# Last phase of a two-layer MetaFormer kernel: the back ring of PSUM banks goes from three banks to two

## The chip, the cores and the metric

The kernel runs on 1 core of one Trainium2 chip. The metric is device time in microseconds (us); lower is better. Engines are named as the profile names them: PE is TensorE's matmul, PEld its weight load, DVE is VectorE, ACT is ScalarE, POOL is GpSimd, SP is SyncE, which only issues transfers here. PSUM, the memory that PE writes, has eight banks in each partition; a matmul output sits in one bank, and DVE or ACT must read it out before PE may overwrite it.

## The reference: what is computed

The input is (8, 96, 128, 128). Two layers follow, each a token mixer and then a feed-forward network (FFN) with a hidden size of 384, both with a residual:

```
x = x + L0_conv(ln_c(x), ...)                      # layer 0: clustering mixer
t = to_tokens(x); t = t + L0_ffn(ln_t(t), ...); x = from_tokens(t)
x = x + L1_conv(ln_c(x), ...)                      # layer 1: convolutions, then pw * gate
t = to_tokens(x); t = t + L1_ffn(ln_t(t), ...); x = from_tokens(t)
# ffn: y = q_acc(q_mul(relu(q_acc(q_mul(x) W1) + b1)) W2) + b2, with fp8 and fp16 rounding
```

Layer 1's mixer ends with a 1x1 convolution (`pw_w`) whose result is multiplied by the normalised input of the mixer.

## The kernel before, in words

There are three phases: A (layer 0), B (depthwise convolutions of layer 1) and C (the 1x1 convolution, the gate, and the FFN of layer 1). Only phase C is touched. It runs from about 3025 us to the end.

Phase C works through 32 units (`NQ`) of 4096 tokens, each in 8 groups `k` of 512 tokens. A *step* `i` overlaps two units: the front work of unit q = i + 1 and the FFN of unit i. A step has 9 *slots*, s = 0 to 8 (`FFN_SLOTS`). The steps i = 0 to 30 have both kinds of work; step -1 has only front work and step 31 only the FFN. All engines run their own instruction streams strictly in the order written, and meet at semaphores.

In slot s each engine issues, in this order:

- PE: `q8` of group s+1 (four transposing matmuls, L1409), `hidden` of group s (three matmuls of 512 columns, L272), `pw` of group s (L1577), `turn` of group s-1 (four transposes, L1586), `c` of group s-1 (four transposes, L1596), `y` of group s-1 (three matmuls, L1423).
- ACT: the copy `q8c` of group s+1 (L296), the copy `h16` of `hidden` of group s (L307), in all slots but 1 four normalising activations (L1394), the copy `y16` of group s-1 (L1436).
- DVE: `hq` of group s (L229 three times, L233 once), `gate` of group s (L1653), `x4` of group s-1 (L1663), `y16b` of group s-1 (L1442), statistics (L178), and as its last instruction `out` of group s-1 (L1682), which reads the bank that `c` wrote.

Slots 7 and 8 are irregular. Slot 7 has no `q8`. Slot 8 has the `q8` of group 0 of the next unit, and no `hidden` and no `pw`. Slot 0 has no `turn`, `c`, `y`. Where a text here says "the end of DVE's slot", it means the end of that slot's `out`.

The bank that each PE group writes is given out by `Ring` in rotation. The list of uses is fixed: 24 uses of the back ring in a step (`q8`, `c`, `y`), 16 of the front ring (`pw`, `turn`). Use n takes bank n modulo the number of banks, and `Ring.before` names the use of that same bank just before it; PE then waits, before the first matmul of use n, for the event that says that the earlier use was read out. For `q8` that event is `q8c`, for `y` it is `y16` (both ACT), for `c` it is `out` (DVE). `hidden` has its own three banks (`C_hid`), used once per slot, so `hidden` of group s also waits for `h16` of group s-1. The 24 back uses in order, with s the slot, are: `q8`1 in slot 0; then in slots 1 to 6 `q8`(s+1), `c`(s-1), `y`(s-1); `c`6, `y`6 in slot 7; `q8`0 of the next unit, `c`7, `y`7 in slot 8.

Of the kernel before, what the change touches and what calls it, by code (L numbers as in the profile page):

```python
# [5 lines left out]
F32 = mybir.dt.float32  # L6
# [9 lines left out]
P = 128  # L16
# [1429 lines left out]
def phase_c(nc, consts, pw_t, w1, b1, w2, b2, x2_dram, x3_dram, y3_dram, out_dram):  # L1446
# [3 lines left out]
    with ExitStack() as ctx:  # L1450
        sb = lambda n, s, d: ctx.enter_context(nc.sbuf_tensor(n, s, d))
        sem = lambda n: ctx.enter_context(nc.semaphore(n))
        front_uses, back_uses = [], []
# [28 lines left out]
        gated = sb("C_gated", [C, 2, CH], F32)  # L1482
        outq = sb("C_outq", [C, RB, W], F32)
        front = Ring(front_uses, [ctx.enter_context(nc.psum_tensor(f"C_fbank{p}", [P, 512], F32)) for p in range(2)])
        back = Ring(back_uses, [ctx.enter_context(nc.psum_tensor(f"C_bbank{p}", [P, 512], F32)) for p in range(3)])
        ff = RowFeedForward(nc, ctx, "C_", ev, back, xT_flat, wts, idb)
        HR = RB // 2

# [251 lines left out]
def metaformer_kernel(nc, x, consts, wf_t, wf, bf, wv_t, bv, wp_t, bp, alpha, beta, w1_0, b1_0, w2_0, b2_0,  # L1740
                      gamma, beta_ln, taps, dwb, pw_t, w1_1, b1_1, w2_1, b2_1, out):
    x2_dram = nc.dram_tensor("x2_scratch", [NQ, P, NK * CW], F32, kind="Internal").ap()
    x3_dram = nc.dram_tensor("x3_scratch", [C, B, H, W], F32, kind="Internal").ap()
    y3_dram = nc.dram_tensor("y3_scratch", [C, B, H, W], F32, kind="Internal").ap()
    phase_a(nc, consts, x, wf_t, wf, bf, wv_t, bv, wp_t, bp, alpha, beta, w1_0, b1_0, w2_0, b2_0,
            gamma, beta_ln, x2_dram, x3_dram)
    phase_b(nc, taps, dwb, x3_dram, y3_dram)
    phase_c(nc, consts, pw_t, w1_1, b1_1, w2_1, b2_1, x2_dram, x3_dram, y3_dram, out)
# [54 lines left out]
```

## Time and profile before

| | |
|---|---|
| time, median of 3 runs | 4256.6 us (4250.14 to 4260.43) |
| profiled execution: time, span | 4258.63 us, 4256.8 us |
| mean granted clock of TensorE | 0.887 of full |
| busy over the span | PE 78%, DVE 71%, ACT 63%, POOL 33% |
| phase C, 3400 to 3800 us (400 us) | PE 315.85, DVE 334.19, ACT 336.51 us busy, clock 0.95 |

The time is 1.8 us more than the span. Busy shares are averages over phases with different limits, so phase C is to be read from its own stretch: there PE, DVE and ACT are each busy 79 to 84% of the time, and none is saturated. A granted clock of 1.00 is 2.4 GHz and one of 0.50 is 1.2 GHz; a value between is a stretch that held both.

### The profile page before, as it was taken

How to read it: one execution, taken by the hardware profiler on the slowest of the kernel's cores; microseconds unless marked ns; L12 is line 12 of the kernel's file. 1: busy time of each engine (PE TensorE's matmuls, PEld its weight loads, DVE VectorE, ACT ScalarE, POOL GpSimd, SP SyncE). 2: the span in 40 equal slices, each digit the busy share in tenths (PEclk: the TensorE clock that was granted, in tenths of full speed). 3: DMA queues.
4: the chain of work that ended last, by engine and by line, in shares of the span. 5: the costliest groups of instructions: out<-in, count | busy, mean ns of one | idle time of the engine just before them, and what ended most of it. 6: DMA issues, size and time to landing. Idle time of an engine off the chain costs nothing. (4 is left out here: it accounts for less than half of the span.)

```text
span 4256.8 us, 81198 instructions
## 1 busy us (share of the span) xinstructions
PE 3309.3 (78%) x26660; PEld 2549.8 (60%) x26660; DVE 3027.4 (71%) x7852; ACT 2686.4 (63%) x5250; POOL 1408.0 (33%) x1892
## 2 busy tenths in 40 slices
PE   6767777676776777767669999999788777778787
PEld 5556555555555555555549999999544444444443
DVE  4888888888888888888842222222388788778787
ACT  2567667676676776766752222222388788888887
POOL 3555555555555555555310000000022221212221
PEclk8888788888888887888879999999799999999998
DMA  3133232332323323222146656656766565666562
GB/s 62 44 75 83 67 77 61 75 83 68 75 65 78 83 61 75 71 72 68 53 111 163 168 160 164 166 161 165 183 178 179 151 178 156 174 170 171 155 175 77
DMA packets 733857, 489.89 MB, mean 115 GB/s; under 512 B 420796, under 2 KB 712956, under 8 KB 721276
## 3 DMA queue, kind: packets, MB, share of 16 engines
q1 hardware_dynamic: 733564, 486.32, 43.3%
q8 instruction: 143, 2.34, 0.2%
q14 instruction: 150, 1.23, 0.1%
HBM read 284.42 MB, written 201.33 MB: 114 GB/s over the span
## 5 line engine op out<-in xcount | busy, mean ns | idle before, releaser
L1722 POOL TENSOR_SCALAR C_var<-C_st 128x16 f32<-128x16 f32 x64 | 13.2, 207 | 1775.8 <-DVE C_st L178 1775.8
L1264 PE MATMUL B_ps_row<-B_g,B_z 128*128 128x128 f32 x4608 | 555.8, 277 | 0.6 <-ACT B_g L1296 0.6
L1264 PEld LDWEIGHTS B_ps_row<-B_g,B_z 128*128 128x128 f32 x4608 | 532.2, 193 | 0.7 <-ACT B_g L1296 0.7
L178 DVE BATCH_NORM_STATS2 A_st<-A_xT 128x6 f32<-128x192 f32 x1536 | 446.7, 350 | 30.7 <-ACT A_xT L764 17.3
L166 POOL TENSOR_TENSOR A_rstd<-A_var,A_expo 128x16 f32<-128x16 f32 x128 | 454.2, 3549 | 23.8 <-POOL A_var L163 23.6
L1357 DVE TENSOR_TENSOR B_mid<-B_ps_row,B_row_bias 128x512 f32<-128x512 f32 x192 | 132.8, 692 | 457.7 <-PE B_ps_row L1264 447.7
L1394 ACT ACTIVATE C_q<-C_xT,C_shift,C_rstd 128x96 fp8e5<-128x96 f32 x1024 | 392.0, 457 | 41.5 <-POOL C_shift L1729 41.0
L307 ACT ACTIVATE A_h<-A_hid 128x1536 f16<-128x1536 f32 x256 | 370.6, 1448 | 55.4 <-PE A_hid L272 51.6
L307 ACT ACTIVATE C_h<-C_hid 128x1536 f16<-128x1536 f32 x256 | 370.5, 1447 | 20.0 <-PE C_hid L272 12.9
L794 ACT ACTIVATE A_xc<-A_xT,A_shift,A_rstd 128x96 f32<-128x96 f32 x1024 | 379.4, 462 | 0.0
L229 DVE TENSOR_SCALAR A_hq<-A_h,A_b 128x512 f16<-128x512 f16 x768 | 240.8, 369 | 178.9 <-ACT A_h L307 178.6
L608 PE MATMUL A_fbank<-A_big_w,A_xq 97*128 97x112 f32 x2048 | 305.4, 313 | 66.3 <-DVE A_pabd L976 64.6
L608 PEld LDWEIGHTS A_fbank<-A_big_w,A_xq 97*128 97x128 f32 x2048 | 297.0, 227 | 93.6 <-DVE A_pabd L976 79.4
L1308 ACT ACTIVATE B_y<-B_ps_col,B_col_bias 128x512 f32<-128x512 f32 x192 | 132.0, 687 | 318.2 <-PE B_ps_col L1275 318.2
L1577 PE MATMUL C_fbank<-C_y3q,C_pw 96*96 96x512 f32 x512 | 280.9, 632 | 48.6 <-DVE C_gated L1653 24.3
L229 DVE TENSOR_SCALAR C_hq<-C_h,C_b 128x512 f16<-128x512 f16 x768 | 224.6, 349 | 122.9 <-ACT C_h L307 80.5
L288 PE MATMUL A_bbank<-A_w,A_hq 128*128 128x96 f16 x3072 | 219.4, 234 | 98.7 <-ACT A_x3h L805 85.8
L288 PEld LDWEIGHTS A_bbank<-A_w,A_hq 128*128 128x128 f16 x3072 | 197.7, 115 | 145.5 <-issue 112.7
L296 ACT ACTIVATE A_q8c<-A_bbank 96x512 bf16<-96x512 f32 x256 | 150.8, 590 | 197.5 <-PE A_bbank L258 196.2
L691 PE MATMUL A_fbank<-A_pabd,A_simT 128*128 128x384 f32 x512 | 261.2, 646 | 5.2 <-DVE A_xT L983 4.3
L1436 ACT ACTIVATE C_y<-C_bbank 96x512 f16<-96x512 f32 x256 | 150.2, 587 | 160.7 <-PE C_bbank L1423 156.9
L1586 PEld LDWEIGHTS C_fbank<-C_cst,C_gated 96*128 96x128 f32 x1024 | 113.2, 145 | 220.7 <-issue 111.9
(162 smaller groups left out, 7778.4 us busy)
## 6 DMA issues: line engine op xcount, KB each, us to landing
A_xq<-in_x SPq DMA_DIRECT2D x32, 1536.0 KB, 8.9
x_scratch<-A_xT SPq DMA_DIRECT2D x64, 768.0 KB, 3.2
x_scratch<-A_x3h SPq DMA_DIRECT2D x64, 768.0 KB, 5.4
B_z<-x_scratch SPq DMA_DIRECT2D x96, 512.0 KB, 5.0
y_scratch<-B_y SPq DMA_DIRECT2D x96, 512.0 KB, 3.7
C_x3q<-x_scratch SPq DMA_DIRECT2D x32, 1536.0 KB, 9.2
C_y3q<-y_scratch SPq DMA_DIRECT2D x32, 1536.0 KB, 15.5
C_xT<-x_scratch SPq DMA_DIRECT2D x64, 768.0 KB, 14.7
```

Source lines behind the costliest of these rows:

```text
L166: m = pool.tensor_tensor(rstd[:, o:o + n], var[:], expo[:, 0:n], ALU.pow)
L178: return dve.bn_stats(st[:, n:n + 2, :].rearrange("p t s -> p (t s)"), x[:, n * C:(n + 2) * C].rearrange("p (t c) -> p c t", t=2))
L229: r = dve.tensor_scalar(self.hq[:, b, s], self.h16[:, b, s], self.w["b1"][:, j:j + 1], 0.0, ALU.add, ALU.max)
L288: m = pe.matmul(bank[:, t * C:(t + 1) * C], self.hq[:, b, s:s + P], self.w["w2"][:, j, :], start=(j == 0), stop=(j == NJ - 1))
L296: act.activation(self.q8c[:, k % 2, :], self.ring.bank("q8", k)[0:C, 0:CH], ACT.Copy).then_inc(self.ev["q8c"], 1)
L307: act.activation(self.h16[:, k % 2, :], self.hid[:, :], ACT.Copy).then_inc(ev["h16"], 1)
L608: m = pe.matmul(bank[:, t * BIGN:(t + 1) * BIGN], xq[q.buf(NX)][:, n * P:(n + 1) * P], big_w[:, :], start=True, stop=True)
L691: pe.matmul(front.bank("out", k)[:, 0:CW], simT[q.buf(2)][:, k, :], pabd[:], start=True, stop=True).then_inc(ev["out_full"], 1)
L794: m = act.activation(xc3[:, k // 4, t % (NT // 2), :], xT[u.buf(NB)][:, t * C:(t + 1) * C], ACT.Identity, scale=rstd3[:, t:t + 1], bias=sh ...
L1264: m = pe.matmul(ps_row[h][:, b * P:(b + 1) * P], z[c.buf(NB)][:, h * HB + b, d:d + W], g[c.buf(2)][:, d, :], start=(d == 0), stop=(d == 2))
L1394: m = act.activation(self.q8[:, t, :], x[:, t * C:(t + 1) * C], ACT.Identity, scale=self.rstd[:, t:t + 1], bias=self.shift[:, t:t + 1], sa ...
L1577: pe.matmul(rows(front.bank("pw", k)[0:C, 0:CH]), pw[:], group(y3q[q.buf(2)], k), start=True, stop=True).then_inc(ev["pw_full"], 1)
```

## The change

The back ring of phase C gets two banks in place of three; one bank of PSUM is left unused. No instruction of any engine is added, dropped or reordered. What changes is which bank each of the 24 back uses writes, and so which earlier use PE waits for before it.

```diff
         front = Ring(front_uses, [ctx.enter_context(nc.psum_tensor(f"C_fbank{p}", [P, 512], F32)) for p in range(2)])
-        back = Ring(back_uses, [ctx.enter_context(nc.psum_tensor(f"C_bbank{p}", [P, 512], F32)) for p in range(3)])
+        back = Ring(back_uses, [ctx.enter_context(nc.psum_tensor(f"C_bbank{p}", [P, 512], F32)) for p in range(2)])
         ff = RowFeedForward(nc, ctx, "C_", ev, back, xT_flat, wts, idb)
```

PE in slot 3 of a step, before. Names in brackets are the semaphores waited for; `C_out` is raised by DVE's `out`, `C_q8c` and `C_y16` by ACT's copies, `C_hq` and `C_gate` by DVE, `C_norm2` and `C_h16` by ACT, `C_x1` by DVE's `x4`:

```order
L1409 MATMUL C_bbank1<-C_idb,C_q8 96x128 [waits C_norm2,C_q8c]
L272 MATMUL C_hid<-C_q8c,C_w1 128x512 [waits C_h16,C_q8c]
L1577 MATMUL C_fbank1<-C_y3q1,C_pw 96x512 [waits C_gate]
L1586 MATMUL C_fbank0<-C_cst,C_gated 128x96 [waits C_x1,C_gate]
L1596 MATMUL C_bbank2<-C_cst,C_xT0 96x128 [waits C_out,C_x1]
L1423 MATMUL C_bbank0<-C_hq,C_w2 96x512 [waits C_y16,C_hq]
```

The same slot of PE, after:

```order
L1409 MATMUL C_bbank1<-C_idb,C_q8 96x128 [waits C_norm2,C_out]
L272 MATMUL C_hid<-C_q8c,C_w1 128x512 [waits C_h16,C_q8c]
L1577 MATMUL C_fbank1<-C_y3q1,C_pw 96x512 [waits C_gate]
L1586 MATMUL C_fbank0<-C_cst,C_gated 128x96 [waits C_x1,C_gate]
L1596 MATMUL C_bbank0<-C_cst,C_xT0 96x128 [waits C_y16,C_x1]
L1423 MATMUL C_bbank1<-C_hq,C_w2 96x512 [waits C_q8c,C_hq]
```

The wait for `C_out` (DVE's `out` of group s-2, the last instruction of DVE's slot s-1) has moved from `c`, the fifth group of the slot, to `q8`, the first. `c` now waits for `C_y16` of group s-2, and `y` for the `C_q8c` of its own slot.

All back uses of a step, worked out from the list above (the group's event in brackets):

| PE group | waits, three banks | waits, two banks |
|---|---|---|
| slot 0: `q8`1 | `q8c` of `q8`0 | `out` 7, end of DVE's slot 8 of the step before |
| slot 1: `q8`2 | `out` 7 | `y16` 7 |
| slot 1: `c`0, `y`0 | `y16` 7, `q8c`1 | `q8c`1, `q8c`2 |
| slots 2 to 6: `q8`(s+1) | `q8c`(s) | `out`(s-2), end of DVE's slot s-1 |
| slots 2 to 6: `c`(s-1), `y`(s-1) | `out`(s-2), `y16`(s-2) | `y16`(s-2), `q8c`(s+1) |
| slot 7: `c`6, `y`6 | `q8c`7, `out`5 | `out`5, `y16`5 |
| slot 8: `q8`0 of the next unit | `y16`5 | `out` 6, end of DVE's slot 7 |
| slot 8: `c`7, `y`7 | `out`6, `y16`6 | `y16`6, `q8c`0 of the next unit |

## Rows read from the trace of the kernel before

**Rows 1.** The page's first line.

```profile
span 4256.8 us, 81198 instructions
```

**Rows 2.** Waits from 3000 us on: who waited for whom, us in total, times, longest.

```profile
PE C_bbank L1596 <- DVE C_outq L1682: 102.6, 185, 2.4
...
DVE C_y16b L1442 <- ACT C_y L1436: 70.8, 41, 3.2
```

**Rows 3.** Chain that ended last, 3600 to 3660 us: start, us, what.

```profile
3654.00 0.14 issue
3654.13 0.61 PE C_bbank L1596 x4
```

**Rows 4.** Timeline, slot 6: start, us, engine, line, instruction, [idle before <-releaser].

```profile
3643.67 0.39 PE L1409 MATMUL C_bbank<-C_idb,C_q 128*96 128x128 bf16 x4 [0.31 <-ACT C_q L1394]
...
3644.10 0.59 ACT L296 ACTIVATE C_q8c<-C_bbank 96x512 bf16<-96x512 f32 x1
...
3644.55 1.02 PE L1577 MATMUL C_fbank<-C_y3q,C_pw 96*96 96x512 f32 x2
...
3644.75 1.45 ACT L307 ACTIVATE C_h<-C_hid 128x1536 f16<-128x1536 f32 x1
...
3645.41 0.49 PE L1586 MATMUL C_fbank<-C_cst,C_gated 96*128 96x96 f32 x4
...
3646.24 0.88 DVE L229 TENSOR_SCALAR C_hq<-C_h,C_b 128x512 f16<-128x512 f16 x3 [0.18 <-ACT C_h L307]
...
3646.65 0.81 PE L1423 MATMUL C_bbank<-C_hq,C_w 128*96 128x512 f16 x3
...
3648.69 0.34 DVE L1442 TENSOR_SCALAR C_y16b<-C_y,C_b 96x512 f16<-96x512 f16 x1
...
3649.49 0.68 DVE L1682 TENSOR_TENSOR C_outq<-C_bbank,C_y16b 96x512 f32<-96x512 f32 x1
```

**Rows 5.** Timeline, `out` that ends a step, then one step later.

```profile
3621.12 0.67 DVE L1682 TENSOR_TENSOR C_outq<-C_bbank,C_y16b 96x512 f32<-96x512 f32 x1
...
3652.14 1.53 ACT L1394 ACTIVATE C_q<-C_xT,C_shift,C_rstd 128x96 fp8e5<-128x96 f32 x4
...
3653.32 0.67 DVE L1682 TENSOR_TENSOR C_outq<-C_bbank,C_y16b 96x512 f32<-96x512 f32 x1
...
3656.05 0.35 DVE L1442 TENSOR_SCALAR C_y16b<-C_y,C_b 96x512 f16<-96x512 f16 x1 [1.61 <-ACT C_y L1436]
...
3656.40 1.45 ACT L307 ACTIVATE C_h<-C_hid 128x1536 f16<-128x1536 f32 x1
...
3656.86 0.68 DVE L1682 TENSOR_TENSOR C_outq<-C_bbank,C_y16b 96x512 f32<-96x512 f32 x1
...
3659.65 1.43 ACT L307 ACTIVATE C_h<-C_hid 128x1536 f16<-128x1536 f32 x1
```

**Rows 6.** Timeline, stretches of phase C at a granted clock of 0.50.

```profile
3364.86 0.88 PE L1586 MATMUL C_fbank<-C_cst,C_gated 96*128 96x96 f32 x4 [8.51 <-DVE C_gated L1653]
...
3366.38 1.49 PE L1423 MATMUL C_bbank<-C_hq,C_w 128*96 128x512 f16 x3
...
3367.90 0.59 ACT L1436 ACTIVATE C_y<-C_bbank 96x512 f16<-96x512 f32 x1 [10.13 <-PE C_bbank L1423]
...
3619.45 0.63 PE L1409 MATMUL C_bbank<-C_idb,C_q 128*96 128x128 bf16 x4
...
3621.15 1.50 PE L1577 MATMUL C_fbank<-C_y3q,C_pw 96*96 96x512 f32 x2
...
3621.39 1.45 ACT L307 ACTIVATE C_h<-C_hid 128x1536 f16<-128x1536 f32 x1 [0.63 <-PE C_hid L272]
```

**Rows 7.** Windows: stretch, length, busy us of PE, PEld, DVE, ACT, POOL; clock, DMA, GB/s.

```profile
3616.50:3618.00 1.50, 0.17 (x3) 0.05 (x2) 1.50 (x5) 1.01 (x3) 0.00 (x0) 1.00 0.73 186
3618.00:3619.50 1.50, 1.50 (x8) 0.96 (x9) 0.30 (x1) 0.00 (x0) 0.00 (x0) 0.73 1.15 284
...
3652.50:3654.00 1.50, 0.30 (x4) 0.12 (x2) 1.50 (x6) 1.17 (x4) 0.00 (x0) 1.00 0.75 175
```

## The prediction, made before the changed kernel ran

> **What bounds the kernel now.** I read the waits from 3000 us on first, then the chain of waits through one step, then the timeline of that step, because busy shares mislead here: PE, DVE and ACT all have idle time, so the order in which they hand work to each other decides. The span is 4256.8 us [rows 1]; the profiled execution took 4258.63 us, 2 us above the median of 4256.6, so a difference worked out against the one holds for the other within 0.1%.
>
> In the waits, PE's longest wait on DVE in phase C is at `c`, for `out`: 102.6 us in 185 waits [rows 2]. That wait stands late in PE's slot, and mostly it costs nothing. The timeline of slot 6 shows why [rows 4]: `q8` starts at 3643.67, `h16` at 3644.75 and ends at 3646.20, and DVE starts its slot with `hq` at 3646.24. The `out` that ended DVE's slot before was over at 3646.06, which is 3646.24 less the 0.18 us that DVE then waited. So PE and ACT made `hidden` and `h16` of slot 6 *while DVE was still in slot 5*. DVE is idle 0.18 us between two slots. Its own work in a slot is 3649.49 + 0.68 - 3646.24 = 3.93 us. The reader is to see this overlap: it is what the third bank pays for.
>
> A whole step, from the `out` that ends one to the `out` that ends the next, takes 3656.86 + 0.68 - (3621.12 + 0.67) = 35.75 us [rows 5].
>
> **The change, part by part.** Instructions stay; only waits move. In slots 2 to 6 `q8`(s+1) now waits for `out`(s-2), and `hidden`(s), `pw`(s) and the rest of PE's slot stand in line behind it. `hidden` itself needs nothing new, but PE issues in order. DVE's next slot begins with `hq`(s), which needs `h16`(s), which needs `hidden`(s). So the loop closes: DVE ends slot s-1, PE does `q8` and `hidden`, ACT does `h16`, and only then can DVE start slot s.
>
> The gap that DVE then sees, at the full clock:
> - from the end of `out` to PE's start: 0.14 us, as where `c` waited for just this event [rows 3];
> - from the start of `q8` to the start of `h16`: 3644.75 - 3643.67 = 1.08 us [rows 4];
> - `h16`: 1.45 us, and 0.04 us to `hq` [rows 4].
>
> That is 2.71 us, so a slot takes 2.71 + 3.93 = 6.64 us. Is anything else later than that? `y`(s-1) follows `q8` by 3646.65 - 3643.67 = 2.98 us or less, so it ends by 3.9 us of the slot; ACT's `y16` comes after `h16` (over at 2.67) and four activations of 1.53 us together [rows 5], at about 4.2, and is over at 4.85. DVE wants it at 2.71 + (3648.69 - 3646.24) = 5.16 [rows 4]. It fits, with 0.3 us to spare. The new wait of `y` on `q8c` is met at 0.14 + 0.43 + 0.59 = 1.16 [rows 4]. So the other moved waits cost nothing.
>
> Now the step, slot by slot, from the `out` that ends the step before:
> - Slots 0 and 1: `q8`1 waits for `out`7, so `h16`0 starts at 1.22; `h16`1 starts 3659.65 - 3656.40 = 3.25 later [rows 5], and ends at 5.92; `hq` of group 1 at 5.96; DVE's 3.93 gives 9.89 us. `q8` of group 2 waits for an ACT copy long done.
> - Slots 2 to 6: 5 x 6.64 = 33.20 us.
> - Slot 7 has no `q8`, so PE and ACT prepare it during slot 6: 3.93 us or a little less, 3.9.
> - Slot 8: today 3656.86 + 0.68 - (3653.32 + 0.67) = 3.55 us, limited by `y`7 and its copy [rows 5]. Now `q8` and `turn` stand between `out`6 and `c`, and ACT's four activations fall behind the late `q8c` and before `y16`: `q8c` over at 1.16, activations at 2.7, `y16` at 3.3, `y16b` at 3.35 where today it starts at 3656.05 - 3653.99 = 2.06. That is +1.3: 4.85 us.
>
> Sum 9.89 + 33.20 + 3.9 + 4.85 = 51.8 us against 35.75, so +16.1 us a step. There are 31 full steps: +499 us. The last step has shorter slots for DVE and a loop that ACT and PE already limit in part, so its cost lies between 0 and 16 us; I take 12. Sum at the full clock: +511 us, 4770 us. Phases A and B and the load at the start of C stay.
>
> **The clock.** In phase C before, the granted clock falls now and then. After a stretch in which PE was busy 0.17 us of 1.5, it was 0.73 in the next 1.5 us, falling from 1.00 to 0.50 within it; one step later, 0.30 busy of 1.5 brought no fall [rows 7]. Such holes come once in a step now. With the change PE works for 3.4 us and then waits 3.3 us in each of five slots of a step, so I expect falls in most slots. At the low level a slot is dearer: `q8` to `h16` takes 3621.39 - 3619.45 = 1.94 us, 0.86 more [rows 6]. And PE's own work stretches: `pw` 3621.15 - 3619.45 = 1.70 after `q8`, `turn` 1.72 later (an estimate, twice the 3645.41 - 3644.55 = 0.86 of [rows 4]), `y` 1.52 later and `y16` another 1.52 [rows 6]. With 0.14 in front, `y16` starts at 6.60 and `y16b` at 7.23; from there to the end of `out` it is 3649.49 + 0.68 - 3648.69 = 1.48 us [rows 4]. A slot wholly at the low level takes 8.7 us. For the step: 5 x 8.7 = 43.5; slots 0 and 1 some 12.4, slot 7 some 6.1, slot 8 some 5.8 (the same distances, with `y` of slots 1 and 7 late too): 67.8 us, +16 on top of 51.8. So the clock term lies between 0 and 31 x 16 = +496 us. The nearest rows say neither end: each fall meets a burst of work, in which PE's busy share rises again. I take a little under half, +230 us.
>
> Forecast: 4258.6 + 511 + 230 = 5000 us.
>
> On this the Trainium skill has a word, "TensorE: Matmul & The Clock Gate", section "A second HAM failure mode: psum-queue depth-cycling": when PE idles briefly between groups of matmuls because it cycles through PSUM banks, the clock swings between its two levels. The trace of before shows such swings only singly. By that rule the clock term is not zero, and it would speak for a value inside the bounds, not for another sum.
>
> **Rivals.**
>
> 1. *Full clock throughout.* The serial loop comes, but the holes do not bring the clock down: 4770 us. For it: the hole of 0.30 us busy in 1.5 that did no harm [rows 7]. Against it: PE's idle stretch grows to 3.3 us and comes five times as often.
>
> 2. *Low clock nearly throughout.* 4770 + 496 = 5266 us. For it: PE's idle stretch is as long as its work. Against it: at the low level PE would be busy most of the time, which in phase C has always brought the clock back.
>
> 3. *The wait is only moved and stays hidden.* PE waits for `out` today as well, 102.6 us in total [rows 2], and the same event merely stops PE earlier in the slot. If DVE's next slot did not depend on what stands behind `q8`, the cost would be the moved instructions' 1 us in a few slots, or nothing: 4260 us. Against it: `hq`(s) needs `h16`(s), and DVE's reserve today is 0.18 us, not 2.7 [rows 4].
>
> 4. *Faster.* `c` and `y` no longer wait for `out` but for ACT copies that are done early. `y` comes earlier, and DVE's waits for `y16`, 70.8 us in 41 waits [rows 2], go: 4258.6 - 71 = 4188 us. It decides only if the wait at `q8` is hidden as in rival 3; the place is slot 8, where `c`7 today waits for `out`6. Against it: there `q8` now waits for that same `out`, in front of `c`, so the gain is eaten where it arises.
>
> The Trainium skill holds a finding for rival 3: in "TensorE: Matmul & The Clock Gate", section "HAM oscillation — how this bites in real kernels", double buffering of PSUM brought one kernel no further gain. By that, taking a bank away would cost next to nothing. The rows here speak against it, since DVE is idle only 0.18 us between slots now and PE works a slot ahead of it.
>
> **How the numbers follow.** The forecast, a serial loop with a mixed clock (4850 to 5170), 0.66. Rival 1 (around 4770) 0.15, rival 2 (around 5266) 0.13, rival 3 0.04, rival 4 0.02. The range from 4790 to 5220 leaves out rivals 3 and 4 and the outer halves of 1 and 2. What a measurement here can tell from no change is about 0.2%, 8 us. Slower by more: 0.96; within it: 0.02; faster: 0.02.
>
> **What would show it.** In the profile after: PE's wait for `out` moves from L1596 to `q8` (L1409) in slots 0, 2 to 6 and 8, with 160 to 220 waits; DVE's idle before `hq` (L229) for `h16` grows by 31 x 6 x 2.5, some 470 us or more; DVE's slots come every 6.6 us, or up to 8.7 where the clock is low, instead of every 4; slot 7 still follows slot 6 without a gap; the granted clock in phase C falls from 0.95 to 0.7 or 0.8. Phases A and B end at the same times. It is wrong if `hidden` starts before `out`(s-2) is over, if the step stays under 45 us, or if the clock term is outside 0 to 500 us.

## The result, and the profile after

| | before | after |
|---|---|---|
| time, median (4 runs each, same chip) | 4258.5 us (4250.1 to 4263.1) | 4921.4 us (4910.7 to 4924.5) |
| span of the profiled execution | 4256.8 us | 4919.1 us |
| mean granted clock | 0.887 | 0.818 |

The changed kernel is slower: 1.1555 times the time of before, 95% interval 1.1529 to 1.158. That is +663 us where the forecast was +741 (5000 us).

The page of after, its first line and the clock (40 equal slices of the span, tenths of full speed):

```profile
span 4919.1 us, 81205 instructions
...
PEclk8888888888888888869999998777777777777777
```

The first 24 slices and part of the next are phases A and B. The clock there reads 8 and 9 but for one slice, much as before, and SP's first transfers of phase C start at 3025.18 us (3025.10 before). So all of the loss lies in phase C, where the clock now reads 7 in every whole slice. A granted clock of 0.74 over a long stretch is a mixture of the two levels, 1.00 and 0.50.

The same 400 us of phase C as in the small table of before (stretch, length, then busy us of PE, PEld, DVE, ACT, POOL; clock, DMA, GB/s):

```profile
3400.00:3800.00 400.00, 272.17 (x1087) 150.06 (x1086) 214.13 (x543) 219.42 (x382) 51.32 (x56) 0.74 0.39 110
```

DVE worked 214 us of 400 where it worked 334. Every engine is less busy, the transfers run at 110 GB/s, and nothing has become saturated: this is what a loop that passes work from engine to engine looks like.

Waits from 3000 us on (engine, its output and line, whom it waited for, us in total, times, longest):

```profile
DVE C_hq L229 <- ACT C_h L307: 636.9, 222, 7.6
...
ACT C_q8c L296 <- PE C_bbank L1409: 518.4, 223, 3.5
PE C_bbank L1409 <- issue: 459.2, 188, 3.4
...
DVE C_y16b L1442 <- ACT C_y L1436: 145.7, 151, 2.2
...
PE C_bbank L1409 <- DVE C_outq L1682: 89.6, 34, 3.3
```

PE now waits at `q8`, and before it waited at `c` [rows 2]. The view puts 34 of those waits down to DVE's `out` and 188 to "issue": `out` ends about 0.1 us ahead of the start of `q8`, and the view often names no releaser. The sum is the telling number. The table of the change gives `out` to seven `q8` in each of steps 1 to 30, and to six in step 0 (its slot 0 has no earlier `out` to wait for) and in step 31 (its slot 8 has no `q8`): 30 x 7 + 2 x 6 = 222 = 188 + 34. In all 222 cases `q8` starts 0.10 us after `out` ends.

One slot at the low clock, where the timeline in [rows 4] shows one of before (start, us, engine, line, instruction, idle before and its releaser):

```profile
4031.13 0.67 DVE L1682 TENSOR_TENSOR C_outq<-C_bbank,C_y16b 96x512 f32<-96x512 f32 x1
...
4031.90 0.63 PE L1409 MATMUL C_bbank<-C_idb,C_q 128*96 128x128 bf16 x4 [2.24 <-issue]
...
4032.33 1.49 PE L272 MATMUL C_hid<-C_q8c,C_w 96*128 96x512 bf16 x3
...
4033.61 1.92 PE L1577 MATMUL C_fbank<-C_y3q,C_pw 96*96 96x512 f32 x2
...
4033.85 1.45 ACT L307 ACTIVATE C_h<-C_hid 128x1536 f16<-128x1536 f32 x1 [0.69 <-PE C_hid L272]
...
4035.34 0.88 DVE L229 TENSOR_SCALAR C_hq<-C_h,C_b 128x512 f16<-128x512 f16 x3 [3.53 <-ACT C_h L307]
...
4036.81 1.49 PE L1423 MATMUL C_bbank<-C_hq,C_w 128*96 128x512 f16 x3
...
4038.33 0.59 ACT L1436 ACTIVATE C_y<-C_bbank 96x512 f16<-96x512 f32 x1 [1.60 <-PE C_bbank L1423]
...
4038.96 0.35 DVE L1442 TENSOR_SCALAR C_y16b<-C_y,C_b 96x512 f16<-96x512 f16 x1 [1.09 <-ACT C_y L1436]
4039.76 0.67 DVE L1682 TENSOR_TENSOR C_outq<-C_bbank,C_y16b 96x512 f32<-96x512 f32 x1
```

Read it as a loop. `out` is over at 4031.80, `q8` starts 0.10 us later, then `hidden`, then `h16`, and only then `hq`: DVE stood idle 3.53 us, where it stood 0.18 us in [rows 4]. The second part of the slot is late too: `y` takes 1.49 us at this clock, so `y16b` starts 7.16 us after `out`. From `out` to `out` it is 8.63 us.

The chain that ended last, over the same slot (start, us, what), says it without the engines beside:

```profile
4029.66 2.24 issue
4031.90 0.63 PE C_bbank L1409 x4
4032.53 1.28 PE C_hid L272 x3
4033.82 1.71 PE C_fbank L1577 x2
4035.52 0.64 PE C_fbank L1586 x4
4036.16 0.85 PE C_bbank L1596 x4
4037.01 1.28 PE C_bbank L1423 x3
4038.30 2.24 issue
```

Six PE groups in a row and then 2.24 us in which PE can do nothing. A chain that names PE all the way may look like a bound by PE; the repeated "issue" of the same length, right in front of `q8`, is the wait for `out`.

Distances between the ends of `out`, a mean over steps 1 to 30, in us:

| | slots 0+1 | 2 | 3 | 4 | 5 | 6 | 7 | 8 | median step |
|---|---|---|---|---|---|---|---|---|---|
| before | 9.11 | 4.01 | 4.00 | 4.10 | 4.11 | 4.11 | 3.82 | 3.85 | 35.7 |
| after | 11.39 | 7.56 | 7.22 | 7.49 | 7.44 | 7.59 | 3.96 | 5.43 | 57.5 |
| forecast, full clock | 9.89 | 6.64 | 6.64 | 6.64 | 6.64 | 6.64 | 3.9 | 4.85 | 51.8 |

Slot 7, which has no `q8`, still follows without a gap, `hq` starting 0.09 us after `out`:

```profile
4046.94 0.67 DVE L1682 TENSOR_TENSOR C_outq<-C_bbank,C_y16b 96x512 f32<-96x512 f32 x1
...
4047.70 0.88 DVE L229 TENSOR_SCALAR C_hq<-C_h,C_b 128x512 f16<-128x512 f16 x3
```

### The profile page after: what moved, and what is told of

Its sections match the earlier page's. It is cut to its first block and busy times, and to the rows that moved or that the text cites. A ratio compares the mean times of both kernels' runs of the same rounds, so it can differ in the third digit from the quotient of the medians.

```text
span 4919.1 us, 81205 instructions
## 1 busy us (share of the span) xinstructions
PE 3635.7 (74%) x26660; PEld 2725.6 (55%) x26660; DVE 3045.9 (62%) x7852; ACT 2719.4 (55%) x5250; POOL 1404.8 (29%) x1892
## 5 line engine op out<-in xcount | busy, mean ns | idle before, releaser
L229 DVE TENSOR_SCALAR C_hq<-C_h,C_b 128x512 f16<-128x512 f16 x768 | 225.2, 349 | 653.5 <-ACT C_h L307 636.9
L1409 PE MATMUL C_bbank<-C_idb,C_q 128*96 128x128 bf16 x1024 | 129.6, 264 | 548.7 <-issue 459.2
L1409 PEld LDWEIGHTS C_bbank<-C_idb,C_q 128*96 128x96 fp8e5 x1024 | 96.5, 154 | 713.4 <-issue 713.3
L296 ACT ACTIVATE C_q8c<-C_bbank 96x512 bf16<-96x512 f32 x256 | 151.3, 591 | 518.4 <-PE C_bbank L1409 518.4
L1577 PE MATMUL C_fbank<-C_y3q,C_pw 96*96 96x512 f32 x512 | 410.8, 898 | 24.7 <-DMA C_y3q<-y_scratch 23.8
L1586 PEld LDWEIGHTS C_fbank<-C_cst,C_gated 96*128 96x128 f32 x1024 | 163.6, 197 | 239.3 <-issue 196.2
L272 PE MATMUL C_hid<-C_q8c,C_w 96*128 96x512 bf16 x768 | 293.0, 504 | 1.3 <-ACT C_h L307 1.2
```

What stands on the lines that cost most here:

```text
L229: r = dve.tensor_scalar(self.hq[:, b, s], self.h16[:, b, s], self.w["b1"][:, j:j + 1], 0.0, ALU.add, ALU.max)
L272: m = pe.matmul(self.hid[:, j * CH:(j + 1) * CH], self.w["w1"][:, j * P:(j + 1) * P], self.q8c[:, k % 2, :], start=True, stop=True)
L1409: m = pe.matmul(bank[0:C, t * P:(t + 1) * P], self.q8[:, k * TPC + t, :], self.idb[:, :], start=True, stop=True)
L1577: pe.matmul(rows(front.bank("pw", k)[0:C, 0:CH]), pw[:], group(y3q[q.buf(2)], k), start=True, stop=True).then_inc(ev["pw_full"], 1)
L1586: m = pe.transpose(front.bank("turn", k)[:, t * C:(t + 1) * C], gated[:, k % 2, t * P:(t + 1) * P], cst[0:C, 0:C])
```

## The experiments

Each was run on one chip together with the kernel before, whose median there was 4254.0 us (the first four), 4255.2 (the next three) or 4256.5 (the last two), and the ratios are against that. Two theories stand against each other. *Order*: the loss comes from the wait for `out` in front of `q8`, with `hidden` behind it. *Room*: the loss comes from there being one bank less. A second question is how much of the loss is the clock.

### The wait alone, with three banks

On the kernel before. The rotation over three banks stays, and PE additionally waits before each `q8` for the event that two banks would have asked for.

```diff
 # in pe_q8
+        name, unit, pos = self.gate_ring.before(step, "q8", k)
+        if begun(unit):
+            pe.wait_ge(ev[name], ev.at(name, unit, pos))
 # in phase_c
+        ff.gate_ring = Ring(back_uses, back.banks[0:2])
```

> Three banks as before, and one wait more: q8 waits also for the event that it would wait for with two banks (out of group s-2 in slots 2 to 6, out 7 in slot 0, out 6 in slot 8). The banks of c and y and their waits stay as before. Theory (the place of the wait makes the cost): same time as the changed kernel, 4921 us, within 20, and DVE slots of 6.6 to 8.6 us. Rival (it is the number of banks, that is the later waits of c and y on ACT's copies, or the banks themselves): near 4259, at most 4300 us.

Measured: 4957.1 us (4953.6 to 4967.9), ratio 1.1657 (1.1634 to 1.1681). The waits from 3000 us on:

```profile
DVE C_hq L229 <- ACT C_h L307: 644.2, 218, 7.7
...
PE C_bbank L1412 <- DVE C_outq L1686: 587.8, 222, 3.6
```

With all three banks in place the whole loss is there, with the same count of 222, this time all put down to `out`. Room is refuted. (Rivals 3 and 4 of the prediction, a hidden wait and a gain, had fallen with the result itself.) The kernel is 36 us slower than the one with two banks, outside the 20 us that I had allowed. The timeline shows where:

```profile
4022.04 0.67 DVE L1686 TENSOR_TENSOR C_outq<-C_bbank,C_y16b 96x512 f32<-96x512 f32 x1
...
4022.96 0.63 PE L1412 MATMUL C_bbank<-C_idb,C_q 128*96 128x128 bf16 x4 [2.39 <-DVE C_outq L1686]
```

From the end of `out` to `q8` it is 0.25 us here, 0.10 with two banks, in each of the 222 cases, and 222 x 0.15 = 33 us. The trace's records of PE show what stands in between: with two banks one semaphore instruction waits for both events of `q8`; here there are two, and the one with `out` comes first, so the other still has to be issued after `out` is over.

### The wait in three of the slots

The same kernel, with the wait before `q8` of groups 3, 4 and 5 only, that is in slots 2, 3 and 4.

```diff
-        if begun(unit):
+        if begun(unit) and k in (3, 4, 5):
```

> As the run with the wait alone, but the extra wait stands only at the q8 of groups 3, 4 and 5, so in slots 2, 3 and 4. Theory of a serial loop slot by slot: each slot with the wait takes about 7.4 us in place of 4.0, so 3 x 31 x 3.4 = 316 us, 4575 us, and somewhat less (4540) if the clock stays up more; slots 5 and 6 stay at 4.1 us. Rival (one wait per step is enough to put the whole pipeline out of step): 4700 us or more.

Measured: 4600.6 us (4594.0 to 4614.5), ratio 1.0809 (1.0791 to 1.0827), +347 us where 316 was expected. Slots 2, 3 and 4 take 7.84, 7.74 and 7.58 us; slots 5 and 6 take 4.27 and 4.09, slots 0+1 9.01, as before. The loss is local: each slot with the wait pays for itself, and the others hardly do (slot 5, right behind, 0.16 us). 347 us over 31 x 3 slots is 3.7 us each (3.4 expected).

### Two banks, shared out another way

On the kernel after. `q8` and `y`, both read by ACT, share one bank; `c`, read by DVE, has the other. Now no `q8` waits for `out`; it waits for `y16`(s-2), the last ACT copy of the slot before.

```diff
+class Shared:
+    def __init__(self, uses, banks):
+        self.parts = {}
+        for stages, bank in ((("q8", "y"), banks[0]), (("c",), banks[1])):
+            ring = Ring([u for u in uses if u[0] in stages], [bank])
+            for stage in stages:
+                self.parts[stage] = ring
...
+        back = Shared(back_uses, back.banks)
```

> Two banks as in the changed kernel, but not in rotation: q8 and y share one bank, c has the other alone. c waits for out of group s-2 as before, q8 of group s+1 waits for y16 of group s-2, y for the q8c of its own slot. Theory: q8 no longer waits for DVE's last instruction; its new event is ACT's last of the slot before, which costs 0.45 us a slot (1.35 + 1.43 + 0.58 + 0.12 + 1.08 = 4.56 in place of 4.1) and 0.8 at slot 0, so 31 x 3.3 = 100 us: 4360 us, between 4300 and 4420. Rival (two banks are too few however they are given out): above 4800 us.

Measured: 4352.5 us (4345.8 to 4358.0), ratio 1.0235 (1.0217 to 1.0253). Slots 2 to 6 take 4.36 to 4.76 us, a step 38.6, where 4.56 a slot was expected. Two banks thus cost 99 us rather than 663, by nothing but who shares with whom. What is left is a shorter loop, which the timeline shows:

```profile
3642.59 0.57 ACT L1452 ACTIVATE C_y<-C_bbank 96x512 f16<-96x512 f32 x1
...
3643.26 0.40 PE L1425 MATMUL C_bbank<-C_idb,C_q 128*96 128x128 bf16 x4 [1.18 <-ACT C_y L1452]
...
3645.83 0.88 DVE L245 TENSOR_SCALAR C_hq<-C_h,C_b 128x512 f16<-128x512 f16 x3 [0.62 <-ACT C_h L323]
```

`q8` starts 0.10 us after `y16` is over, and `h16`, which stands behind it, is 0.62 us too late for DVE.

### `hidden` ahead of `q8`, two banks

On the kernel after. PE issues `hidden`(s) ahead of `q8`(s+1), and ACT issues `h16`(s) ahead of `q8c`(s+1). The wait for `out` stays, but `hidden` no longer stands behind it.

```diff
 # PE's slot
+                    if i.real and s < NK:
+                        ff.pe_hidden(pe, i, s)
...
-                    if i.real and s < NK:
-                        ff.pe_hidden(pe, i, s)
 # ACT's slot: act_hidden moved ahead of act_q8 in the same way
```

> The changed kernel with two neighbours exchanged: PE issues hidden of group s ahead of q8 of group s+1, and ACT the copy h16 ahead of the copy q8c. The wait for out stays at q8. Theory (it costs what stands behind it): hidden and h16 no longer stand behind the wait, so DVE starts hq at once, and what is left is the late y: activations and y16 fall behind the late q8c, y16b at about 3.5 us of the slot in place of 2.45, slots of 5.0 us; 4450 us, between 4350 and 4550. Rival (PE's wait itself is the loss, whatever stands behind): near 4900 us.

Measured: 4512.2 us (4498.7 to 4518.5), ratio 1.0596 (1.0571 to 1.062). A slot at the full clock, from 4036.01 + 0.67 to 4040.95 + 0.67, takes 4.94 us:

```profile
4036.01 0.67 DVE L1682 TENSOR_TENSOR C_outq<-C_bbank,C_y16b 96x512 f32<-96x512 f32 x1
...
4036.72 0.88 DVE L229 TENSOR_SCALAR C_hq<-C_h,C_b 128x512 f16<-128x512 f16 x3
4036.78 0.39 PE L1409 MATMUL C_bbank<-C_idb,C_q 128*96 128x128 bf16 x4 [1.58 <-issue]
...
4040.14 0.35 DVE L1442 TENSOR_SCALAR C_y16b<-C_y,C_b 96x512 f16<-96x512 f16 x1 [0.89 <-ACT C_y L1436]
4040.95 0.67 DVE L1682 TENSOR_TENSOR C_outq<-C_bbank,C_y16b 96x512 f32<-96x512 f32 x1
```

`q8` waits for `out` exactly as in the kernel after, and `hq` starts at once all the same. So the wait costs what stands *behind* it. More than half of the loss is gone: 258 us are left of 663. The rest is the second loop, `out`, `q8`, ACT's activations, `y16`, `y16b`, and a clock of 0.86 in the same 400 us, where it is 0.74 in the kernel after and 0.95 in the kernel before. DVE's idle time has moved from `hq` to `y16b` (83.0 us and 253.1 us in the waits, where the kernel after has 636.9 and 145.7).

### The same exchange with three banks

The two moves of the experiment before, on the kernel before.

> The kernel before, three banks, with the same exchange: hidden of group s ahead of q8 of group s+1 on PE, h16 ahead of q8c on ACT. In the chain of before the normalising activations release q8 and q8 stands ahead of hidden. Theory: that link goes, slots 4 to 6 fall from 4.10 to at best 3.93 us, a gain of up to 31 x 5 x 0.15 = 23 us, 4235 to 4255 us. Rival (ACT's own work bounds these slots): no change, 4258 us, or slower by a few us because q8c comes later.

Measured: 4273.4 us (4270.6 to 4276.3), ratio 1.0041 (1.0027 to 1.0054): a miss, since 4235 to 4255 was expected. Slots 2 to 5 came down to 3.83 to 3.94 us as expected, but slot 6 takes 5.10 (4.11 before) and slot 8 takes 4.39 (3.85). The timeline of slot 6:

```profile
3652.42 0.44 POOL L1729 TENSOR_TENSOR C_shift<-C_less,C_rstd 128x16 f32<-128x16 f32 x1 [0.18 <-POOL C_rstd L1726]
...
3652.98 1.54 ACT L1394 ACTIVATE C_q<-C_xT,C_shift,C_rstd 128x96 fp8e5<-128x96 f32 x4 [1.38 <-POOL C_shift L1729]
...
3655.03 0.35 DVE L1442 TENSOR_SCALAR C_y16b<-C_y,C_b 96x512 f16<-96x512 f16 x1 [1.19 <-ACT C_y L1436]
```

The faster slots bring ACT to slot 6 before POOL has finished `C_shift`, a term of the normalisation of the next unit. ACT stands 1.38 us at its activations, and `y16` stands behind them. It is the lesson of the main change once more, on another engine: something that comes late, waited for ahead of something that others need.

### Filler matmuls: what of the loss is the clock

On the kernel after. PE fills its idle time with matmuls into the spare bank whose results nobody reads; they add work and take no wait away. Six of 512 columns in each of six slots, then ten.

```diff
+        spare = ctx.enter_context(nc.psum_tensor("C_spare", [P, 512], F32))
+        filler = sb("C_filler", [P, 512], BF16)
 # PE's slot, behind y
+                    if i.real and s in (1, 2, 3, 4, 5, 8):
+                        for _ in range(6):      # 10 in the second kernel
+                            pe.matmul(spare[:, :], idb[:, :], filler[:, :], start=True, stop=True)
```

> The changed kernel, with six extra matmuls (128x128 by 128x512, bf16, into the bank that is left unused, results not read) after y in slots 1 to 5 and 8, where PE would wait for out. They fill some 1.3 us of the wait at the full clock. Theory (serial loop plus clock): the granted clock in the last phase rises from 0.74 to above 0.9 and the clock term of about 170 us goes, less what the fillers delay: 4750 to 4830 us. Rival (the slots of 8.6 us have another cause): clock up, time still 4900 or more.

Measured: 4824.3 us (4820.9 to 4845.2), ratio 1.1345 (1.1317 to 1.1373), inside the expected range. The clock of the 400 us rose to 0.86, not above 0.9:

```profile
3400.00:3800.00 400.00, 299.27 (x1416) 164.56 (x1414) 225.96 (x575) 229.98 (x404) 53.54 (x56) 0.86 0.40 111
```

> As the run with six fillers, with ten (some 2.2 us at the full clock, 4.3 us at the half). Theory: the clock stays up wholly, 1.00 in the last phase, slots of 6.6 us throughout: 4750 to 4780 us. If a filler group at the half clock delays the next q8, some slots of 8 us or more are left and the time is above that with six.

Measured: 4759.9 us (4752.9 to 4776.4), ratio 1.1195 (1.1172 to 1.1218). More work, and 161 us *less* time than the kernel after (158 when each is set against the kernel before on its own chip). The same 400 us as above:

```profile
3400.00:3800.00 400.00, 312.27 (x1630) 166.56 (x1629) 231.17 (x595) 235.06 (x417) 56.80 (x60) 0.95 0.40 113
```

The clock is 0.95, as it was before the change and not 1.00 as expected, and DVE is still busy only 231 us. All 155 slots 2 to 6 of steps 0 to 30 now take less than 6.8 us, with a mean of 6.59; the median step takes 52.1. One of them:

```profile
4031.81 0.67 DVE L1688 TENSOR_TENSOR C_outq<-C_bbank,C_y16b 96x512 f32<-96x512 f32 x1
...
4032.58 0.40 PE L1409 MATMUL C_bbank<-C_idb,C_q 128*96 128x128 bf16 x4 [1.21 <-issue]
...
4033.66 1.45 ACT L307 ACTIVATE C_h<-C_hid 128x1536 f16<-128x1536 f32 x1
...
4035.14 0.88 DVE L229 TENSOR_SCALAR C_hq<-C_h,C_b 128x512 f16<-128x512 f16 x3 [2.67 <-ACT C_h L307]
...
4035.73 2.32 PE L1619 MATMUL C_spare<-C_filler,C_idb 128*128 128x512 bf16 x10
...
4038.39 0.67 DVE L1688 TENSOR_TENSOR C_outq<-C_bbank,C_y16b 96x512 f32<-96x512 f32 x1
```

DVE's gap is 2.67 us and the slot 6.58 us. This kernel comes close to the prediction's sum at the full clock, built and timed; in slots 2 to 6 of steps 1 to 30 no time at the low level is left in it.

### Two kernels with the activations moved one slot later

If the exchange with three banks lost its gain in slot 6, then its activations should come one slot later. Both kernels have the exchange (`hidden` and `h16` first) and this edit; the first has three banks, the second two, shared out as above.

```diff
-LN_AT = {6: (1, 0), 7: (1, 1), 8: (1, 2), 0: (0, 3), 2: (0, 4), 3: (0, 5), 4: (0, 6), 5: (0, 7)}
+LN_AT = {7: (1, 0), 8: (1, 1), 0: (0, 2), 1: (0, 3), 2: (0, 4), 3: (0, 5), 4: (0, 6), 5: (0, 7)}
```

> Three banks, hidden and h16 first as in the run before with three banks, and the eight groups of normalising activations moved one slot later where POOL's terms came too late: slots 7, 8, 0, 1 in place of 6, 7, 8, 0 (2 to 5 stay). With hidden first, slots 2 to 5 took 3.83 us in place of 4.1, but slot 6 took 5.10 because ACT waited 1.38 us for POOL. Theory (that wait ate the gain): slot 6 falls to 3.83 as well, the step from 36.7 to some 35.0 us against 35.74 before, 4225 to 4245 us. Rival (the later activations delay hidden of group 1 or y of group 0): slots 0 and 1 grow by over 1 us, 4260 us or more.

Measured, three banks: 4227.3 us (4222.0 to 4228.7), ratio 0.9928 (0.9914 to 0.9941). Slots 3 to 6 all take 3.83 us, slot 2 takes 4.01. The reason given for the miss holds. It is 29 us faster than the kernel before beside it, a gain of 0.7%.

> Two banks, given out as q8 and y on one and c on the other, with hidden and h16 first and the activations moved as in the run beside it. Theory (a bank's number matters only through what stands behind its wait): q8 waits for y16 of the slot before, but hidden no longer stands behind it, so the 0.45 us a slot go and the time is that of the three-bank version beside it, within 15 us: 4225 to 4260 us, no slower than the kernel before. Rival (two banks always cost): 4320 us or more.

Measured, two banks: 4206.4 us (4199.8 to 4210.4), ratio 0.9886 (0.987 to 0.9901). With one bank of PSUM unused, this is the fastest kernel of the study, 50 us below the kernel before beside it and 715 below the kernel after. I had expected 4225 to 4260 us, within 15 us of the three banks; it is 21 us faster than they are, a miss. The two windows (three banks, then two):

```profile
3400.00:3800.00 400.00, 321.07 (x1722) 178.44 (x1720) 328.98 (x858) 333.71 (x608) 95.01 (x88) 0.93 0.61 170
```

```profile
3400.00:3800.00 400.00, 323.05 (x1782) 173.19 (x1781) 340.78 (x890) 342.62 (x621) 99.98 (x90) 0.97 0.63 175
```

The clock is 0.97 in place of 0.93, and slots 0+1 take 8.63 us in place of 9.26. Which of the two brings the other I did not try; that stays open.

## Why the prediction was right

**The bound and the overlap: right.** DVE was idle only 0.18 us between slots, so whatever came later than that was paid for in full. The gap is now 2.67 us at the full clock (2.71 forecast), read in the ten-filler kernel, and 3.53 at the low one, read in the kernel after.

**The wait moves to `q8` and `hidden` stands behind it: right, and shown from three sides.** The wait without the missing bank costs as much and 36 us more (4957). The missing bank without the wait for `out` costs 99 us (4352). The wait with `hidden` taken out from behind it costs 258 us in place of 663 (4512). That the other moved waits cost nothing in slots 2 to 6 fits the full-clock slots, 6.59 us on average (6.64 forecast).

**The serial term, 511 us: right to about 1%, in part because small errors cancel.** The ten-filler kernel took 4760 us, 505 more than the 4255 of before beside it; its median step takes 52.1 us (51.8 forecast), its slots 0+1 9.82 in the median (9.89 forecast). One thing that the prediction had not seen lies in it. Five of the steps of before, four apart, were already long, 44.0 to 44.9 us: there DVE stands for some 8 us ahead of `hq` with no releaser named. They are steps 8, 12, 16, 20 and 24, and the kernel's text says what they share: steps 4 to 27 are a `Fori` loop of six turns with four steps each (`sweep`), and these five are the steps that a jump back leads to. The trace of before has six of DVE's branches at L111, one at the end of each turn. Behind the five that jump back, DVE's next instruction after `out` is recorded 8.4 to 9.2 us after the branch; behind the sixth, which leaves the loop, it is 2.0 us. The waits from 3000 us on, before:

```profile
DVE C_hq L229 <- issue: 40.3, 5, 8.4
```

After (two under this name, the others now among the waits for `h16`, of which the longest is 7.6 us):

```profile
DVE C_hq L229 <- issue: 15.8, 2, 8.4
```

In before, those five steps exceed the mean of the other 25 by 8.7 us on average, in the ten-filler kernel by 6.7, in the kernel after by 5.4. So part of that stop now lies beside the new wait: some 5 x 2.0 = 10 us that the serial term did not cost, and 5 x 3.3 = 16 us in the kernel after. The last step cost 9.6 us in the ten-filler kernel, where 12 were forecast, and 13.0 in the kernel after.

**The clock term, 230 us: the one that was mis-sized.** It measures 4921 - 4760 = 161 us. Its bounds (0 to 496), the sign, and the slot at the low level (8.63 us, 8.7 forecast) were right. The clock in the window fell to 0.74, inside the forecast's 0.7 to 0.8. What failed is that one share, "a little under half", was laid on 16 us in *every* part of the step. The table sets the kernel after against the ten-filler kernel, mean over mean, with the low level's share of the time in the kernel after (worked out from the clock of these stretches in steps 1 to 30):

| us a step | dearest, forecast | found | share at the low level |
|---|---|---|---|
| slots 2 to 6 | 43.5 - 33.2 = 10.3 | 37.3 - 32.9 = 4.4 | 51% |
| slots 0+1 | 12.4 - 9.9 = 2.5 | 11.39 - 11.18 = 0.2 | 50% |
| slot 7 | 6.1 - 3.9 = 2.2 | 3.96 - 3.83 = 0.1 | 9% |
| slot 8 | 5.8 - 4.85 = 1.0 | 5.43 - 4.93 = 0.5 | 85% |

Slots 2 to 6 paid 42% of their dearest, about as weighed. Slot 7 paid next to nothing because the low level hardly fell on it: 9% of its time, at most 24% in any of 30 steps, and its longest was 4.13 us. Whether a slot 7 wholly at the low level would take 6.1 us no run shows. The kernel with three banks and `hidden` first speaks against it: its slot 7 had the low level for about half of the time in steps 0, 12 and 20 and took 3.83 to 3.84 us, as at the full clock. In slots 0+1 the clock cost 1.0 us in the ordinary step (median 10.86 against 9.82), but where DVE's stop falls it cost nothing (15.7 at most, against 17.0), so the mean hardly moved. The third column sums to 5.2 us, some 160 us over 31 steps, which accounts for the 161. Rival 1 left the clock term out (4770 us), rival 2 took it whole (5266); 4921 lies between them, as forecast.

**The two rules of the Trainium skill.** The swing of the clock that "TensorE: Matmul & The Clock Gate" describes in "A second HAM failure mode: psum-queue depth-cycling" is what these runs show: 0.95 before, 0.74 after, and back at 0.95 with fillers in PE's pauses and no wait taken away. What "HAM oscillation — how this bites in real kernels" reports of double buffering without gain did not carry over as a statement on banks: here the number of banks alone does not set the time (two banks gave 4921, 4352 and 4206 us); who must release a bank, and what stands behind the wait, does.

**Of the signs named,** the count of waits, DVE's idle time before `hq` (80.5 us before, 636.9 after: +556, at least 470 forecast), slot 7, the clock, and the unchanged phases A and B all came; the 222 waits are two more than the 160 to 220 named. The label was different from what I had written: most of PE's waits at `q8` read "issue".

## What to carry to other kernels

Taking a buffer out of a rotation does not only shorten the distance of reuse, it changes *whom* each use waits for. List for each use the event before and after, and look for one that is raised last in a slot and is now waited for first. Let uses that the same engine releases early share a bank, and put what the slowest chain needs ahead of the instruction that waits.

When PE begins to pause between bursts, reckon a clock term beside the serial one, and weigh it slot by slot: here slots 2 to 6, in which PE waits and its work is part of the loop, carried 4.4 of the 5.2 us, and slot 7, in which it does not wait, saw little of the low level.

## What the runs showed of the hardware that was not expected

- A second semaphore instruction between the last release and a PE group cost 0.15 us each time (0.25 against 0.10 us from the end of `out` to the start of `q8`, in 222 cases each), 33 us of the 36 between the two kernels.
- Ten matmuls with no use in each of six slots of a step, 2.32 us of PE each time, raised the clock of phase C from 0.74 to 0.95 and made the kernel 161 us faster; six raised it to 0.86, and brought 97 us.
- DVE stops for 7.5 to 8.3 us in the kernel before, and for 7.3 to 8.2 in the kernel after, each time between the last `out` of a turn of the `Fori` loop and the next turn's first instruction: five times for five jumps back, and not at the loop's exit. So the stop goes with the jump; what in the jump takes the time was not tried, and no run has the loop written out.
